# One block for all stages after the setup of a two-layer gated cross-attention kernel

## The reference

```python
x = x + tanh(g_xattn[0]) * L0_xattn(layernorm(x), ctx)   # 16 heads of 96, 4 key/value heads, keys = 375 context rows + 112 own rows
x = x + tanh(g_ffn[0])   * L0_ffn(layernorm(x))          # bf16 product with a 4-bit weight times scales
x = x + tanh(g_xattn[1]) * L1_xattn(layernorm(x), ctx)   # one head of 1024; softmax(Q K^T / 32) @ ctx
x = x + tanh(g_ffn[1])   * L1_ffn(layernorm(x))          # 1024x1024 + bias + low-rank part chosen by a gate
```

## Time and profile before

| what | value |
|---|---|
| median of 3 runs | 2038.38 us (2035.17 to 2041.88) |
| the profiled execution | 2039.67 us, its span 2037.9 us |
| PE busy | 1966.1 us (96%) |
| DVE, ACT, POOL busy | 1037.3, 743.1, 735.4 us |
| mean granted clock | 0.992 |

### The profile page before, as it was taken

The page is one execution under the profiler, slowest core; times in us unless marked ns, Lnnn a source line. Parts: engine busy times, 40 slices in busy tenths (PEclk is TensorE's granted clock), DMA queues, the critical chain, the costliest instruction groups (busy, mean ns, idle before and its releaser), DMA issues. The chain is left out here.

```text
span 2037.9 us, 37346 instructions
## 1 busy us (share of the span) xinstructions
PE 1966.1 (96%) x13954; PEld 1298.7 (64%) x13968; DVE 1037.3 (51%) x1999; ACT 743.1 (36%) x1559; POOL 735.4 (36%) x722
## 2 busy tenths in 40 slices
PE   7999999998999999999999989999999959999998
PEld 3478888884666666666666545666766745666665
DVE  5555545533555555555555654343343436565564
ACT  4411111222555555555555651111111143444442
POOL 0000000111556565655565550011010147667662
PEclk9999999999999999999999999999999979999999
DMA  6533333333222222243222453231322456666661
GB/s 208 144 105 110 99 111 98 119 95 79 65 65 69 64 67 64 68 92 90 64 67 64 116 132 111 63 94 57 82 80 60 145 174 198 196 213 204 191 213 61
DMA packets 313217, 223.86 MB, mean 110 GB/s; under 512 B 247984, under 2 KB 284848, under 8 KB 308896
## 3 DMA queue, kind: packets, MB, share of 16 engines
q1 hardware_dynamic: 281840, 208.87, 35.5%
q10 hardware_dynamic: 31280, 13.64, 2.6%
HBM read 170.76 MB, written 51.65 MB: 109 GB/s over the span
## 5 line engine op out<-in xcount | busy, mean ns | idle before, releaser
L873 POOL TENSOR_TENSOR b_probT<-b_exp,b_probT 128x448 f16<-128x448 f32 (+2 forms) x256 | 265.1, 1038 | 301.8 <-ACT b_probT L935 301.8
L448 POOL TENSOR_TENSOR cT<-ctx_raw,cT 128x375 f16<-128x375 f32 x256 | 224.7, 898 | 132.5 <-ACT cT L443 132.5
L674 PE MATMUL a_pr<-a_yT,proj_q_p 128*128 128x256 f16 x2016 | 223.2, 273 | 0.0
L674 PEld LDWEIGHTS a_pr<-a_yT,proj_q_p 128*128 128x128 f16 x2016 | 197.3, 98 | 23.4
L1068 PE MATMUL b_kv_ps<-wkv_p,cT 128*128 128x384 f16 (+1 forms) x1152 | 210.6, 325 | 0.0
L1003 DVE TENSOR_REDUCE b_nmax<-b_mx_ps 112x2 f16<-112x974 f32 x128 | 149.6, 1169 | 109.5 <-PE b_mx_ps L1080 109.4
L1064 PE MATMUL b_kv_ps<-cT,wkv_p 128*128 128x375 f16 x1152 | 201.2, 326 | 3.7 <-PEq L465 3.7
L1105 PE MATMUL b_s_ps<-b_qT,b_kT 96*128 96x448 f16 (+5 forms) x768 | 189.6, 354 | 3.2 <-DMA b_qT<-b_nrow 2.2
L1120 PE MATMUL b_o_ps<-b_probT,b_v 128*128 128x448 f16 (+5 forms) x768 | 187.3, 351 | 4.4 <-POOL b_probT L873 4.4
L933 ACT ACTIVATE b_exp<-b_s_ps 128x448 f32<-128x448 f32 (+2 forms) x256 | 138.0, 539 | 127.6 <-PE b_s_ps L1105 121.1
L1812 PE MATMUL d_f_ps<-wo_early,d_y3T 128*112 128x512 f16 x768 | 173.8, 379 | 0.0
(11 more groups left out here) (202 smaller groups left out, 2816.2 us busy)
## 6 DMA issues: line engine op xcount, KB each, us to landing
ctx_raw<-in_ctx_t SPq DMA_DIRECT2D x32, 1500.0 KB, 7.9
d_cn_raw<-in_ctx_nat SPq DMA_DIRECT2D x30, 512.0 KB
b_qT<-qk_scratch SPq DMA_DIRECT2D x32, 336.0 KB, 4.5
o_scratch<-b_o SPq DMA_DIRECT2D x128, 84.0 KB, 1.9
qk_scratch<-a_heads SPq DMA_DIRECT2D x70, 144.0 KB, 2.1
x_scratch<-c_x SPq DMA_DIRECT2D x14, 512.5 KB, 3.6
raw<-in_x SPq DMA_DIRECT2D x14, 512.0 KB, 3.8
wkv_p<-in_x SPq DMA_DIRECT2D x14, 512.0 KB, 3.2
```

Of the source, the lines that this page charges most:

```text
L448: pool.tensor_tensor(cT[:, p, 1, k, 0:S], ctx_raw[:, k, :], cT[:, p, 0, k, 0:S], ALU.subtract).then_inc(split_lo, 1)
L674: last = mm(pr[:, n % PR, 0:GT * P], w[:, b, k, at * P:(at + 1) * P], yT[:, g % 2, a, k, :], start=(x == 0 and k == 0), stop=(x == 2 and k ...
L873: pool.tensor_tensor(pT[0:m, c, 1, :], ex[0:m, i % 2, :], pT[0:m, c, 0, :], ALU.subtract).then_inc(p_lo, 1)
```

## The change

All instructions of A, B, C and D are now in one block: `a_sync` and its siblings are called at the head of `b_sync`..., those at the head of `c_sync`..., those at the head of D's streams. The block ends after A and after C are gone, and with A's goes the clearing of its semaphores. Ordering that the block ends gave is written as waits. The attention of batch 0 moves from D's slot 0 into C's slot 14: its scores after `f`, its transposed probabilities after the first half of the folded projection, its attend one `m` later. What it needs moves earlier: context of batch 0 split in slot 13, of batch 1 in slot 14, n0 to n2 ahead of the weights, their low parts now by DVE in slot 13; w0 to w2 split at the head of slot 14's vector work, w3 to w7 through slot 14. Stores of tiles 12 and 13 of `tT` move from ACT's to SP's stream. Renames (xin to tiles_in, scored to scored1 and others) are left out below.

```diff
 @@ b_tensor @@
+                    a_tensor(pe)
...
                     for m in range(3 * BLOCK):
+                        if m in (0, BLOCK):
+                            pe.wait_ge(lo, GROUPS * BLOCKS - 2 + m // BLOCK)
                         project(0, 0, m)
+                    pe.wait_ge(lo, GROUPS * BLOCKS)
...
-            STAGED = [("w", k) for k in range(6)] + [("n", c) for c in range(3)] + [("b", 0), ("w", 6), ("w", 7)]
+            STAGED = [("n", c) for c in range(3)] + [("w", k) for k in range(6)] + [("b", 0), ("w", 6), ("w", 7)]
...
@@ c_sync, slot(j, p, s) @@
                         if isinstance(s, int) and s == TILES - 1:
                             sp.wait_ge(wo_done, 2 * s)
                             load_raw(sp, B, 0)
                             for c in range(3):
                                 load_staged(sp, "n", c)
+                            sp.wait_ge(t_stored, 32)
+                            for part in range(2):
+                                sp.dma_start(rowsT[0][:, part, :, :], t_s[part, :, :, 0:Q]).then_inc(tx_loaded[0], 16)
+                            sp.wait_ge(x2_stored[0], 16 * (TILES // 2 - 1))
+                            sp.dma_start(x2_first[:, 0:D + 1], x2_s[0:Q, 0:D + 1]).then_inc(tx_loaded[0], 16)
+                            sp.dma_start(ag_in[:, :, :], wag).then_inc(wag_loaded, 16)
...
+                        if isinstance(s, int) and s == TILES:
+                            load_raw(sp, B + 1, 1)
+                            for k in range(3, 6):
+                                load_staged(sp, "w", k)
+                        if inside(s - 1, TILES):
+                            store_rows(1 - p, s - 1)
+                        if isinstance(s, int) and s == TILES - 1:
+                            for k in range(3):
+                                load_staged(sp, "w", k)
+                        if isinstance(s, int) and s == TILES:
+                            sp.wait_ge(t_stored, 64)
+                            for part in range(2):
+                                sp.dma_start(rowsT[1][:, part, :, :], t_s[part, :, :, Q:2 * Q]).then_inc(tx_loaded[1], 16)
+                            sp.wait_ge(x2_stored[0], 16 * (TILES // 2))
+                            load_biases(sp)
+                            store_turned(sp, s - 2)
                             load_staged(sp, "b", 0)
+                            for k in range(6, KD):
+                                load_staged(sp, "w", k)
+                        if isinstance(s, int) and s == SLOTS - 1:
+                            load_second(sp)
+                            store_turned(sp, s - 2)
...
@@ c_scalar, slot(j, p, s), behind y2T_hi @@
                         if isinstance(s, int) and s == TILES - 1:
+                            for k in range(KD):
+                                split_high(act, 0, B, k)
+                            act.wait_ge(wo_done, 2 * TILES)
+                            for c in range(3):
+                                staged_high(act, "n", c)
...
+                        if isinstance(s, int) and s == TILES:
+                            exponent(act, 0)
+                            for k in range(KD):
+                                split_high(act, 1, B + 1, k)
+                            for k in range(3, 5):
+                                staged_high(act, "w", k)
+                            probs_read(act, 0)
+                            staged_high(act, "w", 5)
+                            act.wait_ge(wb_loaded, 32)
+                            act.activation(wb_p[:, 0, :], b_in[:, :], ACT.Copy, scale=WS).then_inc(wb_hi, 1)
+                            for k in range(6, KD):
+                                staged_high(act, "w", k)
...
@@ c_vector, slot(j, p, s) @@
+                            if isinstance(s, int) and s == TILES:
+                                for k in range(3):
+                                    weight_low(dve, k)
...
+                        if isinstance(s, int) and s == TILES:
+                            softmax_head(dve, 0, 0, 0)
...
+                        if isinstance(s, int) and s == TILES - 1:
+                            for c in range(3):
+                                first_natural_low(dve, c)
+                        if isinstance(s, int) and s == TILES:
+                            softmax_tail(dve, 0)
+                            for k in range(3, 5):
+                                weight_low(dve, k)
                             for h in range(2):
+                                if isinstance(s, int) and s == TILES and h == 1:
+                                    attention_added(dve, 0, 0)
...
+                        if isinstance(s, int) and s == TILES:
+                            weight_low(dve, 5)
...
+                            for k in range(6, KD):
+                                weight_low(dve, k)
...
@@ c_tensor, slot(j, p, s) @@
+                        if isinstance(s, int) and s == TILES:
+                            scores_begun(pe, 0, 0, 0)
+                            scores_ended(pe, 0)
...
+                                    if isinstance(s, int) and s == TILES and m == KD // 2:
+                                        probs_turned(pe, 0)
+                                    if isinstance(s, int) and s == TILES and m == KD // 2 + 1:
+                                        attend1(pe, 0)
...
@@ block D, sync @@
-                for k in range(6, KD):
-                    load_staged(sp, "w", k)
...
+                c_sync(sp)
                 def slot(j, p, s):
                     if inside(s + 1, B):
                         ...
                         load_natural(s + 1)
...
@@ block D, vector, slot(j, p, s) @@
+                    if isinstance(s, int) and s == 1:
+                        dve.wait_ge(bias_loaded, 32)
+                        dve.tensor_scalar(tg_b[:, :], tg_b[:, :], tg[:, 3:4], None, ALU.mult).then_inc(tg_b_ready, 1)
+                        dve.wait_ge(tg_b_ready, 1)
+                        bias_added(dve, 0, 0)
+                    if later(s):
+                        softmax_head(dve, j, p, s)
```

More of the change, by code:

```diff
@@ L167, in early_sem @@
                     return early[-1]
[L169 removed]
+                rows_loaded = [early_sem(f"a_x_loaded{i}") for i in range(2)]
                 y_ready = early_sem("a_y_ready")
@@ new lines, in attention_added @@
+            def attention_added(dve, p, s):
+                for h in range(2):
+                    cols = slice(h * HALF, (h + 1) * HALF)
+                    dve.wait_ge(attended, 2 * s + h + 1)
+                    dve.scalar_tensor_tensor(out=x3[:, cols], in0=a_ps[0:Q, h, :], scalar=tg[0:Q, 2:3],
+                                             in1=rows2[p][:, cols], op0=ALU.mult, op1=ALU.add
+                                             ).then_inc(x3_ready, 1)
+                dve.wait_ge(x3_ready, 2 * s + 2)
+                norm3_measure(dve, x3[:, :], Q, s)
+                wait(dve, y3tr, s)
+                norm3_scaled(dve, y3[:, :], x3[:, :], Q, s).then_inc(y3_ready, 1)
@@ new lines, in probs_read, with scores @@
+            def probs_read(act, s):
+                act.wait_ge(ptr, s + 1)
+                for c, (a, n) in enumerate(CH):
+                    for part in range(2):
+                        o = (part * 3 + c) * Q
+                        act.activation(pT1[0:n, part, c, :], tr1[0:n, 0, o:o + Q], ACT.Copy).then_inc(pT_ready, 1)
+            def scores(pe, p, n):
+                for k in range(KD):
+                    last = mm(s1_ps[0:Q, 0:S], rowsT[p][:, PASSES[n][0], k, :], cT[:, p, PASSES[n][1], k, 0:S],
+                              start=(n == 0 and k == 0), stop=(n == 2 and k == KD - 1))
+                return last
@@ new lines, in scores_begun, with scores_ended, probs_turned @@
+            def scores_begun(pe, j, p, s):
+                pe.wait_ge(split_lo, KD * (s + 1 + B))
+                pe.wait_ge(tx_loaded[p], rows_in(j, p))
+                wait(pe, exped1, s)
+                for n in range(2):
+                    scores(pe, p, n)
+            def scores_ended(pe, p):
+                scores(pe, p, 2).then_inc(scored1, 1)
+            def probs_turned(pe, s):
+                for part in range(2):
+                    pe.wait_ge((p1_hi, p1_lo)[part], s + 1)
+                    for c, (a, n) in enumerate(CH):
+                        o = (part * 3 + c) * Q
+                        last = pe.transpose(tr1[0:n, 0, o:o + Q], pp[:, part, a:a + n], ident[0:Q, 0:Q])
+                last.then_inc(ptr, 1)
@@ new lines, in attend1 @@
+            def attend1(pe, s):
+                pe.wait_ge(cn_lo, 3 * (s + 1))
+                pe.wait_ge(pT_ready, 6 * (s + 1))
+                for h in range(2):
+                    wait(pe, x3_ready, 2 * (s - 1) + h + 1)
+                    for i, (a, b) in enumerate(PASSES):
+                        for c, (_, n) in enumerate(CH):
```

(18 more changed lines are left out.)

402 lines of the change are left out of this document (180 added, 222 removed).

## The result

The changed kernel takes **2033.85 us** (median of 8 runs, 2031.96 to 2037.48), the kernel before 2040.66 (8 runs, 2035.17 to 2046.87): a ratio of 0.997 [0.9959, 0.998]. The forecast was 2026. The time lies at the upper end of the stated range of 2018 to 2034, and the gain is 6.8 us where 12.3 were forecast. (The forecast also started 2.3 us too low: it took the kernel before at 2038.38, the median of its first three runs.) The profiled execution took 2033.91 with a span of 2032.1; PE is busy for 1964.3 us of it, 97%.

What follows compares the result with a forecast made beforehand. The prediction took PE's work as the bound, with holes at block ends and in slot 14 that also lower its clock. Gains of 6.7 and 5.6 make 12.3 off 2039.67, less 1.3 to the median: 2026 us, range 2018 to 2034.

Steps and rivals of the forecast that it cites:

- the stop ahead of `ag`: Start of D: PE idles 20 us before `ag`, which waits for ACT's y3T behind the conversion of batch 1's context rows.
- The first seam: Seam A/B: without the block's end and its hole of 3.70 us, `top_scores` begins earlier; gain 6.7 us (5.0 to 6.8).
- to be too short for the clock to fall: Slot 14 of C: PE idles 2.5 us before y2's transposes and keeps full clock; otherwise 1.5 us comes back.
- The landing of the context rows: Start of D: three loads of batch 1's context rows take 8.91 us from issue to ACT's start.
- the second seam: C and D joined, batch 0's attention in slot 14: slot 2 of D starts at 1706.2, a gain of 5.6 us.
- Its 72 matmuls of B took 14.57: Seam A/B: B's first matmuls took 14.57 us at low clock; without the hole they take 11.5.
- rival (4): Seam A/B: Q and K come late or the 1.2 GHz stretch stays; first gain 2 to 3, 2030 us; chance 0.08.
- 1.3 late: Slot 14 of C: ACT's highs and DVE's weight lows ahead of x2 make y2 1.3 us late, at 1641.6.
- The chain: Start of D: from C's end through t32, w7, tT, stores and context rows to `ag`, 24.9 us; `ag` begins at 1684.7.
- My own bound of 12: Start of D: context rows need up to 12 us to land if the stores ahead of them slow them.
- Rival (3): Start of D: the chain is 5.6 us longer and the stop eats the whole second gain; 2032 us; chance 0.17.
- Rival (2): Start of D: the ACT stop isn't there; second gain 23.1, in all 29.8 us, 2008 us; chance 0.06.

Runs made afterwards that it cites:

- experiment 2: Kernel before with only the second seam changed (C and D in one block, first attention in slot 14), A keeping its own block: 2038.69 us against 2039.74.
- experiment 5: Changed kernel with 12 projection matmuls of batch 1 moved ahead of B's first scores, into PE's wait for the row of maxima: 2031.22 us.
- Experiment 4: Changed kernel with GpSimd's low part of tT in slot 14 moved behind its low part of the probabilities: 2032.70 us.
- experiment 7: Changed kernel with SP waiting until batch 1's context rows have landed before it issues the loads of batch 2: 2031.44 us.
- Experiment 3: Changed kernel with the load of batch 1's context rows moved right behind C's matmuls, ahead of second rows and tile 13's stores: 2023.37 us.
- experiment 6: Changed kernel with ACT's conversion of batch 1's context rows moved behind y3T's high part, in slot 1 of D: 2030.94 us.
- experiments 8: Changed kernel with four edits together: context rows loaded early, ACT converting them behind y3T, GpSimd's low part of tT later, 12 projections ahead of B's scores: 2016.42 us.

## Why the forecast gain was nearly twice the measured one

The holes closed and the stop ahead of `ag` came as forecast; three terms of the sum did not hold. The first seam was put at 6.7 and is worth 4.5. In slot 14 a wait of 2.5 us was taken "to be too short for the clock to fall", and the move of one GpSimd instruction had no term: 3.0 us. The landing of the context rows was put at 8.91 and took 11.4: with the chain around it 2.0 us. Of the 5.6 forecast for the second seam 1.6 are left.

**Seam A/B.** The mechanism held: no hole, 72 matmuls in 11.62 (11.5 forecast), no wait for Q or K, `top_scores` 6.6 earlier counted from the end of A (19.34 to 12.74; 6.7 forecast). The term was mis-sized in two ways. "Its 72 matmuls of B took 14.57" was one trace's value and the largest of three; over the three traces with the old seam `top_scores` stands 18.36 behind the end of A in the mean, so the gain there is 5.6. And 1.6 us of it are given back behind the wait for the row of maxima, where the changed kernel's clock falls. The forecast watched the clock at the hole it removed and not at the next one. Its rival (4) had late Q and K or the old stretch at 1.2 GHz staying, and no rival had a fall at a later wait. (5.6 less 1.6 is 4.0; the table's 4.5 is higher because one of the three traces with the old seam has the fall too.)

Is the fall the change's doing? It came in all seven traces that have the new seam and the wait (40.0 to 40.1 in the table's first column), and in one of three with the old seam: experiment 2 has it (45.07 in spite of the shortest 72 projections), both traces of the kernel before don't. So the same instructions give both levels, and seven against one in three is a hint and no proof that the new seam makes the fall likelier. What decides it stays open; experiment 5 shows what filling the wait gives back, 2.6 us.

**Slot 14 of C.** Of the forecast's 28.2 us from `f` to the end of C, 31.2 were measured, and 3.0 of the missing gain are here. Three steps: y2 "1.3 late" was right for what stands ahead of it (its normalisation starts 8.97 behind `f`, in the two traces of before 7.8 and 8.0), but the instruction itself took 2.53 instead of 0.81, since the diff also moves GpSimd's low part of tT to just behind `norm2_root`. The prediction has no term for that move: 1.7 us. "Too short for the clock to fall" is the step that failed outright: the windows after stand at 0.50 from 1638 to 1644. Transposes and y2T took 3.08 instead of 2.1 (1.0), and the folded projection with what lies in it 16.53 instead of 16.1 (0.4: its first half took 1.4 more at the low clock, and the wait of 0.7 for y2T's low part didn't come). Experiment 4 takes the first away and leaves the second: with a wait of 2.53, just the 2.5 of the forecast, the clock falls all the same (0.50 from 1640 to 1644), and 1.2 to 1.4 of the 1.7 reach the end of C. The windows of the trace after:

```profile
1636.00:1638.00 2.00, 0.00 (x0) 0.00 (x0) 2.00 (x1) 0.00 (x0) 1.91 (x1) 0.91 1.02 418
1638.00:1640.00 2.00, 1.48 (x7) 1.49 (x8) 1.93 (x5) 0.00 (x0) 0.00 (x0) 0.50 0.66 268
...
1642.00:1644.00 2.00, 2.00 (x21) 2.00 (x20) 1.64 (x4) 2.00 (x7) 0.21 (x1) 0.50 1.00 250
```

**Start of D.** The chain is the one forecast, link by link: w7 lands in 4.0 (4.1), and SP reaches the context rows 11.7 after the end of C (its terms add up to 11.6, without handovers). Then the rows take 11.4 to land where I took 8.91: 2.5 us. The chain has 26.9 where 24.9 were forecast; the handovers cost 0.5 less than I gave them. My own bound of 12 had "the stores ahead of them" as its reason; experiment 7 puts 1.9 of the 2.5 on the loads of batch 2 issued behind them (1.6 to 2.3 by the six traces that have them). From `ag` to slot 2 it took 21.29 (21.5 forecast), with the bias sum at 3.03 as taken. Experiment 3 confirms that SP's order is the cause of 9.5 us of the stop, and experiment 6 shows what stands behind ACT.

**The second sum.** 5.6, less 3.0 and 2.0, plus 0.2, is 0.8; the one pair of traces shows 0.9. The rest of the 1.6 comes from the kernel before, whose stretch was 0.9 longer in the mean of three traces than in the one that I worked from.

**The rivals.** Rival (3), the stop eats the whole second gain, comes nearest with 2032; it got 0.17. Its cause was to be a chain 5.6 longer; it is 2.0 longer, and slot 14, to which I had given a bound of +1.5, gave the other 3.0. Rival (2) is experiment 3 in part: with the rows early the time is 2023, not 2008, as `ag` still waits 12.76.

## What to carry to other kernels

When an engine's wait is removed, walk on to its next waits of 2 us and more: at two of them PE's clock fell here, and matmuls behind them took 1.6 us more (six scores and twelve projections) and 1.4 to 2.7 (96 matmuls, 6.89 to 8.16 instead of 5.5). In both traces of the kernel before, the first of the two waits cost no clock. When a transfer ends the chain, look for what is ahead of it in its queue (10.5 us here for moving three loads ahead of a load and a pair of stores that wait for other engines) and for what is issued right behind it (1.9). An instruction that is moved on an idle engine is not free if it lands beside one on the path: 2.12 us on GpSimd made DVE's 0.81 into 2.53.

## What the hardware showed unexpectedly

The granted clock fell to 0.50 behind waits of 2.39 and 2.53 us ahead of the transposes (experiments 8 and 4) and of 2.22 or 2.23 us ahead of B's first scores (0.50 in the trace after), with no longer hole near, and stayed at 1.00 behind the same 2.22 us in both traces of before: the length of the wait alone doesn't tell which. The same three loads took 8.9, 9.5 and 11.4 us from issue to the engine that reads them; the loads issued behind them made the step from 9.5 to 11.4.
